# An LSTM with a conditioned adapter: its largest weight loaded by GpSimd in eight 1 MB transfers, x loaded a block earlier

## The chip, the cores and the metric

The kernel runs on one core of a Trainium2 chip. The metric is the device time of one execution in microseconds (us). An execution under the profiler leaves a trace, whose span is given beside its own time. Engines are named as in the profile: PE is TensorE's matmul (PEld its weight load), DVE VectorE, ACT ScalarE, POOL GpSimd, SP SyncE, which only issues transfers here. A "q" behind a name (SPq) is the engine's sequencer.

## What is computed

x is 16 sequences of 256 steps of 256 numbers, all float32. An LSTM with a start state `cond` runs over it and is added to x; then an adapter whose low-rank weights are made from `cond` is added to that.

```
xz = x @ Wx + b                       # (16, 256, 1024), all steps at once
for t in 0..255:                      # the recurrence
    i, f, o, g = split(xz[:, t] + h @ Wh)
    c = sigmoid(f) * c + sigmoid(i) * tanh(g)
    h = sigmoid(o) * tanh(c)
x = x + all h
c = layernorm(cond) * gamma + beta    # 16 x 256
hid = gelu(c @ W1 + bias1)            # 16 x 256
a1, b1, a2, b2 = split(hid @ W2 + bias2)   # W2 is 256 x 8192; each a 16 x 256 x 8 set
mid = gelu(x @ base_down + (x . a2) . b2)
out = x + mid @ base_up.T + a1 . (b1 . mid)
```

## The kernel before

Each engine runs a program of its own, written out by hand; semaphores join them. The 256 time steps are cut into 32 blocks of 8. A block k does three things at once.

- The recurrence: per step PE adds `h @ Wh` to the seeded gate sums (`z`, `z_o`, L712: 24 matmuls), DVE turns them (L868, L872), ACT takes the tanh of the gates (L422, L428), DVE makes cell and hidden state (L878 to L893). Each needs the one before; the second `h_t` instruction (L893, from `z_o`) ends a step.
- The projection `x @ Wx` for block k+2, in eight matmul pieces (`project`, L502) that PE runs in the idle time of the steps; the table `PIECES` says how many are done before each step of blocks 0, 1 and later ones. DVE adds the bias (`evacuate_projection`, L802), and SP rearranges the result into `seed` with four transfers (`load_seed`, L255). x for it is loaded by SP (`load_x`, L244), turned by PE (`transpose_x`, L483) and copied by ACT (`evacuate_x`, L352).
- The adapter for an earlier block (from block 3 on; L515 to L592).

The adapter's weights are made in the first four blocks by `make_weights`, one copy of which stands in the program of PE, of ACT and of DVE. Layer norm of `cond`, then in block 0 at step 3 `c @ W1` and the GELU that makes `hid`, in steps 4 and 5 base_up is turned. W2 (8.4 MB) is cut into four quarters, which are a2, b1, b2 and a1 in the order in which they are made (`QUARTERS`). From step 11 on, each step multiplies one of a quarter's four parts (L633), so a quarter takes four steps; `w2_loaded` says that its data are there. There are three buffers for the four quarters, so the last one waits for the first one's products (`w_psum`). DVE adds the bias (L920, `w_biased`), and GpSimd carries each finished quarter to its place across partitions with four small transfers (`place_w`, L1020), for which PE waits (`w_placed`) in steps 18 and 22 to turn a2 and b1 (L645), and in block 3 to use b2 and a1.

Before, SP loads W2 (`load_w2`, L272 to L283): 16 pieces in two halves of 64 partitions and 256 KB, in runs of 1 KB, and each half waits until the third one before it has landed (`UNDER_WAY`), so that at most three are under way. SP's order by block:

```
k = 0: W2 pieces 0, 1;  x(3);  W2 pieces 2 to 7, a bias transfer behind four of them;  seed(2)
k = 1: x(4);  W2 pieces 8 to 12;  seed(3)
k = 2: x(5);  W2 pieces 13 to 15;  seed(4)
k > 2: x(k+3);  seed(k+2);  a store
```

GpSimd makes constants, adds h to x once per block (`add_h`, L1001) and places the weights; it issues no loads.

Of the kernel before, what the change touches and what calls it, by code (L numbers as in the profile page):

```python
# [42 lines left out]
UNDER_WAY = 3  # L43
# [9 lines left out]
PIECES = ((0, 0, 0, 2, 2, 4, 5, 7, 8), (0, 1, 2, 3, 4, 5, 6, 7, 8), (0, 1, 2, 3, 4, 5, 6, 7, 8))  # L53
# [5 lines left out]
def lstm_adapter(nc, x, cond, Wx, Wh, b, base_up, base_down, gamma, beta, W1, bias1, W2, bias2, out):  # L59
    ctx = ExitStack()  # L60
    with ctx:
# [36 lines left out]
        w1 = sb("w1", [P, 2, D])  # L98
# [50 lines left out]
        w2_loaded = [[[sem(f"w2_loaded{q}_{i}_{r}") for r in range(2)] for i in range(NQ)] for q in range(4)]  # L149
# [89 lines left out]
        def _(sp):  # L239
# [30 lines left out]
            w2_parts = W2.rearrange("(k p) (q j h n) -> q h k p j n", p=P, q=4, j=NQ, n=W_HALF)  # L270

            def load_w2(piece):  # L272

                n, i = divmod(piece, NQ)
                q, (h, kc) = QUARTERS[n], divmod(i, 2)
                if piece == 3 * NQ:
                    sp.wait_ge(w_psum, 2)
                for r, rows in enumerate((slice(0, P // 2), slice(P // 2, P))):
                    back, half = divmod(2 * piece + r - UNDER_WAY, 2)
                    if back >= 0:  # L280
                        sp.wait_ge(w2_loaded[QUARTERS[back // NQ]][back % NQ][half], 16)
                    sp.dma_start(w2[q][rows, kc, :].rearrange("p (j h n) -> p h j n", j=NQ, n=W_HALF)[:, h],
                                 w2_parts[q, h, kc, rows]).then_inc(w2_loaded[q][i][r], 16)  # L283

            bias_q = bias2.rearrange("(q j n) -> j q n", q=4, j=NQ)

            def load_w_bias(j):
                sp.wait_ge(w_bias_zeroed, 1)
                sp.dma_start(w_bias[32 * j:32 * j + B, :, :], bias_q[j].partition_broadcast(B)).then_inc(w_bias_loaded, 16)

# [13 lines left out]
            sp.dma_start(b1_col[:, :], bias1.rearrange("(k p) -> p k", p=P),  # L304
                         allow_slow_non_contiguous=True).then_inc(w_loaded["w1"], 16)
# [4 lines left out]
            def one_block(k, front):  # L310
                if not k.at_least(1):
                    load_w2(0)
                    load_w2(1)
                if k.plus(3).exists():
                    load_x(k.plus(3))
                for piece in {0: range(2, 8), 1: range(8, 13), 2: range(13, 4 * NQ)}.get(k.k, ()):
                    load_w2(piece)
                    if 2 <= piece < 2 + NQ:
                        load_w_bias(piece - 2)
# [19 lines left out]
        def _(act):  # L339
# [40 lines left out]
            def make_weights(k, s):  # L380

                if k == 0 and s == 3:

                    act.wait_ge(w_loaded["w1"], 32)
# [28 lines left out]
            def one_block(k, front):  # L413
                a, e, done = follower(k), early(k), follower(k.plus(-1))
                for s in range(TB):
# [34 lines left out]
                    if s == 1 and not k.at_least(1):  # L450
                        evacuate_x(k.plus(2))
# [26 lines left out]
        def _(pe):  # L478
# [115 lines left out]
            def make_weights(k, s):  # L594
# [7 lines left out]
                if k == 0 and s == 3:  # L602
                    pe.wait_ge(w_loaded["w1"], 32)
                    pe.wait_ge(cond_t_ready, 1)
                    for i in range(2):
                        for kc in range(2):
                            ins = pe.matmul(aux[:, i * B:(i + 1) * B], w1[:, kc, i * P:(i + 1) * P], c_t[:, kc, :],
                                            start=(kc == 0), stop=(kc == 1))
                    ins.then_inc(hidden_psum, 1)
# [9 lines left out]
                if 0 <= k * TB + s - W_FIRST < 4 * NQ:  # L619
# [9 lines left out]
                    for half in w2_loaded[q][i]:  # L629
                        pe.wait_ge(half, 16)  # L630
# [44 lines left out]
            project(Blk(0, 1), range(6))  # L675
# [5 lines left out]
            def one_block(k, front):  # L681
# [3 lines left out]
                for s in range(TB):  # L685
# [111 lines left out]
        def _(dve):  # L797
# [63 lines left out]
            for q in range(XQ - 1):  # L861
# [34 lines left out]
            def make_weights(k, s):  # L896
# [14 lines left out]
                if 0 <= u < 2 * NQ and not between:  # L911
                    n, h = divmod(u, 2)
                    dve.wait_ge(w_psum, u + 1)
                    if u == 0:
                        dve.wait_ge(w_bias_loaded, 16 * NQ)
# [13 lines left out]
            def one_block(k, front):  # L929
                a, e, f, done = follower(k), early(k), k.plus(2), follower(k.plus(-1))  # L930
                for s in range(TB):
# [25 lines left out]
                    if s == 0 and not k.at_least(1):  # L957
                        evacuate_projection(Blk(0, 1), XQ - 1)
# [25 lines left out]
        def _(pool):  # L984
# [27 lines left out]

            places = {0: a1_t[:, :], 1: w_tmp[:, 1, :], 2: w_tmp[:, 0, :], 3: b2_t[:, :]}
# [10 lines left out]
            def one_block(k, front):  # L1024
                add_h(k)
                for n in {0: (0,), 1: (1, 2), 2: (3,)}.get(k.k, ()):
                    place_w(n)

# [24 lines left out]
```

## Time and profile before

| | us |
|---|---|
| median of 3 runs | 602.32 (600.86 to 602.75) |
| the profiled execution, its own time | 606.49 |
| its span | 604.7 |
| PE busy in the span | 584.7 (97%); 14116 matmul and 14116 weight-load instructions |
| DVE, ACT, POOL busy | 502.5, 384.6, 47.4 |
| mean granted clock of TensorE | 0.994 |

Times of the trace are microseconds from the start of the span. In rows of instructions the first number is the start, the second the time that the merged instructions took, then engine, line, operation and tiles (out<-in); in brackets the idle time of the engine before it and what ended it. In rows of windows each engine has its busy time and its number of instructions; PEclk is the granted share of TensorE's clock, the DMA share the mean busy share of the 16 DMA engines.

### The profile page before, as it was taken

Reading aid. Unit: us, or ns where it says so; the run is one execution under the profiler, and the core shown is the slowest. Engines: PE = TensorE matmul, PEld = TensorE weight load, DVE = VectorE, ACT = ScalarE, POOL = GpSimd, SP = SyncE. Lnnn points to the kernel's source line nnn. Section 1 sums busy time; section 2 is a strip of 40 time slices with the busy share of each in tenths; the row PEclk is TensorE's granted clock in tenths of the full one; section 3 lists DMA queues with packets and bytes.
Section 4 is the critical chain, followed back from the end, with each engine's and each line's share of the span. In section 5 each row is a group of like instructions: output and inputs, shape, how many; then the busy total and the mean of one; then the engine's idle time right before and its main releaser. Section 6 shows DMA issues by size and latency. Waiting matters only on the chain.

```text
span 604.7 us, 34273 instructions
## 1 busy us (share of the span) xinstructions
PE 584.7 (97%) x14116; PEld 440.1 (73%) x14116; DVE 502.5 (83%) x2810; ACT 384.6 (64%) x2155; POOL 47.4 (8%) x91
## 2 busy tenths in 40 slices
PE   8888989999999999999999999999999999999997
PEld 7555557777777777777777777777777777777886
DVE  4667768888888888888888888888888888888874
ACT  2555546666666666666666666666666666666663
POOL 4002122000000000000000000000000000000000
PEclk9989899999999999999999999999999999999999
DMA  7999872123332212323221132332123333212201
GB/s 195 184 179 179 174 148 45 33 37 56 56 56 56 41 27 48 55 56 56 56 42 37 37 55 57 55 56 40 40 35 56 55 56 55 45 37 26 56 21 29
DMA packets 40158, 39.75 MB, mean 66 GB/s; under 512 B 4369, under 2 KB 38977, under 8 KB 40002
## 3 DMA queue, kind: packets, MB, share of 16 engines
q1 hardware_dynamic: 39456, 37.01, 33.7%
q8 instruction: 112, 1.84, 1.4%
q0 software_dynamic: 512, 0.53, 0.5%
q14 instruction: 44, 0.36, 0.3%
q10 hardware_dynamic: 34, 0.02, 0.0%
HBM read 16.05 MB, written 4.19 MB: 33 GB/s over the span
## 4 chain that ended last, share of the span: by engine, by line
PE 93%; DVE 2%; issue 2%; DMA 2%; SPq 0%; ACT 0%; DVEq 0%; ACTq 0%
PE z L712 35%; PE x_bank L502 18%; PE z_o L712 9%; PE aux L531 8%; PE out_bank L558 7%; PE aux L515 3%; PE aux L483 2%; PE out_bank L590 2%; PE aux L538 2%; PE out_bank L633 1%; DMA x_nat<-in_x 1%; DMA seed<-proj 1%; PE out_bank L579 1%; PE x_bank L579 1%; PE x_bank L531 0%
## 5 line engine op out<-in xcount | busy, mean ns | idle before, releaser
L712 PE MATMUL z<-wh,h_t 128*16 128x96 f32 x8160 | 235.5, 249 | 5.4 <-issue 3.4
L712 PEld LDWEIGHTS z<-wh,h_t 128*16 128x16 f32 x8160 | 154.2, 96 | 110.6 <-DVE h_t L893 79.8
L868 DVE STREAM_TRANSPOSE z<-z 128x96 f32<-128x96 f32 x512 | 152.4, 298 | 71.1 <-PE z L712 47.8
L422 ACT ACTIVATE gates<-z 128x48 f32<-128x48 f32 x512 | 108.1, 211 | 122.5 <-DVE z L868 122.3
L502 PE MATMUL x_bank<-wx,x_t 128*128 128x256 f32 x512 | 153.6, 387 | 0.6 <-ACT x_t L352 0.5
L358 ACT ACTIVATE z<-seed 128x96 f32<-128x96 f32 x512 | 126.9, 248 | 4.2 <-DMA seed<-proj 4.2
L712 PE MATMUL z_o<-wh,h_t 128*16 128x64 f32 x4080 | 105.6, 220 | 4.9 <-issue 4.9
L878 DVE SCALAR_TENSOR_TENSOR prod<-gates 128x32 f32<-128x32 f32 x512 | 98.2, 192 | 0.3
L712 PEld LDWEIGHTS z_o<-wh,h_t 128*16 128x16 f32 x4080 | 80.7, 97 | 5.4 <-issue 5.3
L502 PEld LDWEIGHTS x_bank<-wx,x_t 128*128 128x128 f32 x512 | 79.1, 192 | 4.2 <-ACT x_t L352 0.7
L428 ACT ACTIVATE gate_o<-z_o 128x32 f32<-128x32 f32 x256 | 50.6, 198 | 31.7 <-DVE z_o L872 6.4
L362 ACT ACTIVATE z_o<-seed 128x64 f32<-128x64 f32 x256 | 58.3, 228 | 19.3
L872 DVE STREAM_TRANSPOSE z_o<-z_o 128x64 f32<-128x64 f32 x256 | 65.7, 257 | 5.1 <-PE z_o L712 5.0
L1001 POOL TENSOR_TENSOR xp<-x_t,h_t 128x128 f32<-128x128 f32 (+1 forms) x60 | 30.3, 527 | 473.7 <-DVE h_t L893 456.6
L434 ACT ACTIVATE z_o<-z 128x16 f32<-128x16 f32 x256 | 43.0, 168 | 25.6
L802 DVE TENSOR_TENSOR proj<-x_bank,b_all 128x256 f32<-128x256 f32 x128 | 54.0, 422 | 2.4 <-PE x_bank L502 2.3
L883 DVE SCALAR_TENSOR_TENSOR z<-prod 128x16 f32<-128x16 f32 x256 | 46.7, 182 | 8.7
L888 DVE SCALAR_TENSOR_TENSOR gates<-prod 128x32 f32<-128x32 f32 x255 | 46.9, 184 | 0.0
L434 ACT ACTIVATE tanc<-tanc 128x16 f32<-128x16 f32 x256 | 45.6, 178 | 0.0
L893 DVE SCALAR_TENSOR_TENSOR h_t<-gate_o,z_o 128x16 f32<-128x16 f32 x256 | 43.7, 171 | 0.1
L893 DVE SCALAR_TENSOR_TENSOR h_t<-gate_o,tanc 128x16 f32<-128x16 f32 x256 | 43.7, 171 | 0.0
L531 PE MATMUL aux<-xp,down 128*128 128x128 f32 x232 | 43.3, 289 | 0.0
(137 smaller groups left out, 521.9 us busy)
## 6 DMA issues: line engine op xcount, KB each, us to landing
seed<-proj SPq DMA_DIRECT2D x128, 128.0 KB, 4.4
w<-in_L_cond_W SPq DMA_DIRECT2D x33, 256.0 KB, 4.8
x_nat<-in_x SPq DMA_DIRECT2D x32, 128.0 KB, 4.1
out<-y_nat SPq DMA_DIRECT2D x32, 128.0 KB, 4.1
wx<-in_L_cond_Wx SPq DMA_DIRECT2D x2, 256.0 KB, 3.9
wx<-in_L_cond_Wx SPq DMA_DIRECT2D x1, 512.0 KB, 4.8
wh<-in_L_cond_Wh SPq DMA_DIRECT2D x2, 256.0 KB, 5.7
wh<-in_L_cond_Wh SPq DMA_DIRECT2D x1, 512.0 KB, 6.0
```

The lines of the kernel that those rows point to most:

```text
L358: act.activation(z_bank[m][:, 0:GC], seed[buf][:, s, P * m:P * m + GC], ACT.Copy)\
L362: act.activation(o_bank[:, 0:OC].rearrange("p (m c) -> p m c", c=C), seed[buf][:, s, :].rearrange("p (m q) -> p m q", m=NM)[:, :, GC:P], A ...
L422: act.activation(gates[s % 2][m][:, 0:3 * B].rearrange("p (g b) -> p g b", b=B), zt[m].rearrange("p (g c) -> p g c", c=C)[:, :, 0:B], ACT. ...
L434: act.activation(tanc[m], cell[m], ACT.Tanh, scale=0.5).then_inc(tanc_ready[m], 1)
L502: ins = pe.matmul(x_bank[q % 2][:, 0:XW].rearrange("p (m g c) -> p m g c", m=NM, c=C), x_t[f.k % N_X][:, kc, :], wx[:, kc, :].rearrange("p ...
L531: ins = pe.matmul(mid_bank[a.lane][:, cols], lhs, rhs, start=(part == 0), stop=(part == 2))
L712: ins = pe.matmul(dst, h_prev[:, kc, :], rhs, start=False, stop=(kc == 1), skip_group_check=True)
L802: dve.tensor_tensor(proj[f.par][:, q * XW:(q + 1) * XW], x_bank[q % 2][:, 0:XW], b_all[:, q * XW:(q + 1) * XW], ALU.add).then_inc(xz_ready, 1)
L868: dve.transpose(zt[m], z_bank[m][:, 0:GC]).then_inc(turned[m], 1)
L872: dve.transpose(zt_o, o_bank[:, 0:OC]).then_inc(turned_o, 1)
L878: dve.scalar_tensor_tensor(prod[m][:, :], now[:, 0:2 * B], 1.0, now[:, 2 * B:4 * B], ALU.add, ALU.mult).then_inc(prod_ready[m], 1)
L893: dve.scalar_tensor_tensor(h_t[k.par][:, m, s, 0:B], gate_o[:, B * m:B * (m + 1)], 1.0, tanc[m], ALU.add, ALU.mult).then_inc(ht_ready[m], 1)
```

## The change

W2 goes from SP to GpSimd. There are eight transfers of 1 MB, two (one per half of `hid`) for each quarter, in runs of 8 KB; the source has an outer count of 8: row `8 b + a` of a half of W2 goes to partition `16 a + b`. GpSimd waits for the seeds of block 0 and then issues six of them, each behind a bias transfer, which is cut into 8 partitions each (eight transfers where there were four); the last two bias transfers follow, and the two W2 transfers of the last quarter come behind the placing of the first one, without a small one. PE waits for a whole quarter at once. Because the rows of W2 change their partitions, the columns of `hid` must too: ACT writes a copy of W1 with its columns in that order (`w1_turned`, block 0, step 2), and the bias column `b1_col` is loaded in that order by two transfers.

SP, without W2 and its waits, loads x for block 2 ahead of the seeds of block 0, and from block 0 on x for block k+4 instead of k+3. All eight pieces of block 1's projection are done ahead of step 0, block 2's x is turned in step 0 instead of step 1, and block 2's pieces are spread over steps 1 to 7 as the table says.

```
-UNDER_WAY = 3
-PIECES = ((0, 0, 0, 2, 2, 4, 5, 7, 8), (0, 1, 2, 3, 4, 5, 6, 7, 8), (0, 1, 2, 3, 4, 5, 6, 7, 8))
+PIECES = ((0, 0, 2, 3, 3, 4, 5, 7, 8), (0, 1, 2, 3, 4, 5, 6, 7, 8), (0, 1, 2, 3, 4, 5, 6, 7, 8))
...
SP:
-            w2_parts = W2.rearrange("(k p) (q j h n) -> q h k p j n", p=P, q=4, j=NQ, n=W_HALF)
-            def load_w2(piece):
...
-            def load_w_bias(j):
...
+            load_x(Blk(0, 0, 2))
             load_seed(Blk(0, 0))
-            load_x(Blk(0, 0, 2))
...
                 if not k.at_least(1):
-                    load_w2(0)
-                    load_w2(1)
-                if k.plus(3).exists():
                     load_x(k.plus(3))
-                for piece in {0: range(2, 8), 1: range(8, 13), 2: range(13, 4 * NQ)}.get(k.k, ()):
-                    load_w2(piece)
...
+                    load_x(k.plus(4))
+                elif k.plus(4).exists():
+                    load_x(k.plus(4))
ACT:
+                if k == 0 and s == 2:
+                    act.wait_ge(w_loaded["w1"], 48)
+                    halves = "p k (i a b) -> p (k i) a b"
+                    act.activation(w1_turned[:, :, :].rearrange(halves, i=2, a=8),
+                                   w1[:, :, :].rearrange("p k (i b a) -> p (k i) a b", i=2, a=8), ACT.Copy)\
+                       .then_inc(w1_ready, 1)
...
-                    if s == 1 and not k.at_least(1):
+                    if s == 0 and not k.at_least(1):
                         evacuate_x(k.plus(2))
PE:
-                    for half in w2_loaded[q][i]:
-                        pe.wait_ge(half, 16)
+                    if i == 0:
+                        pe.wait_ge(w2_loaded[q], 32)
...
-            project(Blk(0, 1), range(6))
+            project(Blk(0, 1), range(N_PIECES))
...
                             if s == 0:
-                                project(Blk(0, 1), range(6, N_PIECES))
-                            if s == 1:
                                 transpose_x(f, both)
POOL:
+            bias_q = bias2.rearrange("(q j n) -> j q n", q=4, j=NQ)
+            w2_q = W2.rearrange("(k b a) (q n) -> q k a b n", k=2, a=8, q=4)
+            def load_w_bias(i):
+                first = 32 * (i // 2) + B // 2 * (i % 2)
+                pool.dma_start(w_bias[first:first + B // 2, :, :], bias_q[i // 2].partition_broadcast(B // 2))\
+                    .then_inc(w_bias_loaded, 16)
+            def load_w2(n, kc):
+                q = QUARTERS[n]
+                pool.dma_start(w2[q][:, kc, :], w2_q[q, kc]).then_inc(w2_loaded[q], 16)
+            pool.wait_ge(seed_loaded[0], 16 * NQ)
+            for i in range(2 * (NQ - 1)):
+                load_w_bias(i)
+                load_w2(i // 2, i % 2)
+            for i in range(2 * (NQ - 1), 2 * NQ):
+                load_w_bias(i)
...
                 for n in {0: (0,), 1: (1, 2), 2: (3,)}.get(k.k, ()):
                     place_w(n)
+                if k.k == 0:
+                    pool.wait_ge(w_psum, 2)
+                    for kc in range(2):
+                        load_w2(NQ - 1, kc)
```

SP's queue in block 0 before, from the load of base_down on (`w_0` and `w_1` are buffers of W2):

```order
L267 DMA down<-in_L_cond_base_down 128x2x256
L282 DMA w_0<-in_L_cond_W 64x4x256 x3
L282 DMA w_0<-in_L_cond_W 64x4x256 [waits w2_loaded2_0_0]
L244 DMA x_nat<-in_x 128x1x256 [waits xt_psum]
L282 DMA w_0<-in_L_cond_W 64x4x256 [waits w2_loaded2_0_1]
L282 DMA w_0<-in_L_cond_W 64x4x256 [waits w2_loaded2_1_0]
L289 DMA w_bias<-in_L_cond_bias 16x4x512 [waits w_bias_zeroed]
```

The same place in the changed kernel, up to the x of block 1's turn:

```order
L267 DMA down<-in_L_cond_base_down 128x2x256
L244 DMA x_nat<-in_x 128x1x256 [waits xt_psum] x2
L255 DMA seed<-proj 16x8x256 [waits seeded_o,xz_ready,seeded1,seeded0]
L255 DMA seed<-proj 16x8x256 [waits xz_ready] x3
L244 DMA x_nat<-in_x 128x1x256 [waits xt_psum]
```

All W2 and bias transfers have left the queue with their waits, and two loads of x stand together where one did.

GpSimd's program in the changed kernel, from the step of the layer norm that stood right ahead of `add_h` (`xp_early`) before, to the end of block 0:

```order
L989 TENSOR_TENSOR c_stat<-c_stat,neg_half 16x1 [waits ln_step,w_bias_zeroed]
L996 DMA w_bias<-in_L_cond_bias 8x4x512 [waits seed_loaded0]
L1001 DMA w_0<-in_L_cond_W 128x1x2048
...
L996 DMA w_bias<-in_L_cond_bias 8x4x512 x2
L979 TENSOR_TENSOR xp_early<-x_t,h_t 128x128 [waits ht_ready0,xt_ready]
L979 TENSOR_TENSOR xp_early<-x_t,h_t 128x128 [waits ht_ready1]
L1017 DMA w_tmp<-w_nat 128x1x64 [waits w_biased]
L1017 DMA w_tmp<-w_nat 128x1x64 x3
L1001 DMA w_0<-in_L_cond_W 128x1x2048 [waits w_psum]
L1001 DMA w_0<-in_L_cond_W 128x1x2048
```

Where "..." stands, the pair of a bias and a W2 transfer comes five times more; the first placing (`w_tmp`) and the last quarter of W2 share this queue with them.

## Rows read from the trace of the kernel before

**Rows 1.** The page's 40 slices of the span, busy tenths of PE and DMA
```profile
PE   8888989999999999999999999999999999999997
...
DMA  7999872123332212323221132332123333212201
```

**Rows 2.** DVE in order of time: the second h_t instruction of some steps
```profile
19.36 0.17 DVE L893 SCALAR_TENSOR_TENSOR h_t<-gate_o,z_o 128x16 f32<-128x16 f32 x1
38.78 0.17 DVE L893 SCALAR_TENSOR_TENSOR h_t<-gate_o,z_o 128x16 f32<-128x16 f32 x1
41.59 0.17 DVE L893 SCALAR_TENSOR_TENSOR h_t<-gate_o,z_o 128x16 f32<-128x16 f32 x1
57.47 0.17 DVE L893 SCALAR_TENSOR_TENSOR h_t<-gate_o,z_o 128x16 f32<-128x16 f32 x1
62.63 0.17 DVE L893 SCALAR_TENSOR_TENSOR h_t<-gate_o,z_o 128x16 f32<-128x16 f32 x1
65.78 0.17 DVE L893 SCALAR_TENSOR_TENSOR h_t<-gate_o,z_o 128x16 f32<-128x16 f32 x1
83.09 0.17 DVE L893 SCALAR_TENSOR_TENSOR h_t<-gate_o,z_o 128x16 f32<-128x16 f32 x1
102.31 0.17 DVE L893 SCALAR_TENSOR_TENSOR h_t<-gate_o,z_o 128x16 f32<-128x16 f32 x1
119.91 0.17 DVE L893 SCALAR_TENSOR_TENSOR h_t<-gate_o,z_o 128x16 f32<-128x16 f32 x1
```

**Rows 3.** The chain that ended last, 0 to 110 us: start, us, what
```profile
29.11 0.86 issue
...
35.10 2.38 issue
...
58.94 2.52 issue
...
78.62 2.53 issue
```

**Rows 4.** DMA queues: packets, MB, share; the whole span, then 16 to 90 us
```profile
q8 instruction: 112, 1.84, 1.4%
...
q1 hardware_dynamic: 13026, 12.35, 88.5%
...
q8 instruction: 12, 0.20, 1.4%
```

**Rows 5.** Windows between the stalls: PE, PEld, DVE, ACT, POOL, clock, DMA share, GB/s
```profile
37.47:58.94 21.47, 20.23 (x503) 13.10 (x504) 17.40 (x96) 12.49 (x73) 3.56 (x7) 0.92 0.97 175
61.46:78.62 17.16, 17.16 (x376) 10.30 (x375) 14.36 (x74) 9.81 (x55) 2.09 (x4) 0.90 0.94 185
```

**Rows 6.** Windows behind the second and the third stall
```profile
38.66:42.00 3.34, 3.28 (x59) 2.29 (x62) 2.30 (x14) 2.16 (x12) 1.01 (x2) 0.50 0.79 148
62.50:65.90 3.40, 3.40 (x58) 2.31 (x50) 2.54 (x14) 1.65 (x10) 0.00 (x0) 0.51 0.71 162
```

**Rows 7.** Windows of the first loads and of the stretch that loads W2
```profile
0.00:10.00 10.00, 8.94 (x42) 8.17 (x42) 3.77 (x13) 3.02 (x5) 5.98 (x10) 1.00 0.75 240
...
17.00:87.00 70.00, 59.20 (x1443) 39.58 (x1444) 51.02 (x275) 37.48 (x213) 9.47 (x18) 0.95 0.95 181
```

**Rows 8.** ACT in order of time: the first seed
```profile
16.83 0.42 ACT L358 ACTIVATE z<-seed 128x96 f32<-128x96 f32 x2 [4.16 <-DMA seed<-proj]
```

**Rows 9.** POOL and PE in order of time: the first placing, its use
```profile
56.39 2.24 POOL L1020 DMA_DIRECT2D w_tmp<-w_nat  x4 [16.54 <-DVE w_nat L920]
...
68.58 0.44 PE L645 MATMUL aux<-ident,w_tmp 128*128 128x128 f32 x2
```

**Rows 10.** PE in order of time: x for block 4 is turned
```profile
56.64 0.44 PE L483 MATMUL aux<-ident,x_nat 128*128 128x128 f32 x2 [0.36 <-DMA x_nat<-in_x]
```

**Rows 11.** ACT in order of time: a copy of 128x512, step 3's first gates
```profile
8.28 0.63 ACT L399 ACTIVATE wh<-wh 128x512 f32<-128x512 f32 x1 [2.98 <-DMA wh<-in_L_cond_Wh]
...
25.03 0.21 ACT L422 ACTIVATE gates<-z 128x48 f32<-128x48 f32 x1 [0.71 <-DVE z L868]
```

More of the change, by code:

```diff
@@ L97, in lstm_adapter @@
         c_t = sb("c_t", [P, 2, B])
-        w1 = sb("w1", [P, 2, D])
+        w1, w1_turned = sb("w1", [P, 2, D]), sb("w1_turned", [P, 2, D])
         b1_col = sb("b1_col", [P, 2])
@@ L148, in lstm_adapter @@
                     ("wx_g", "wx_if", "wx_o", "wh_g", "wh_if", "wh_o", "b", "down", "up", "ln", "cond", "w1")}
-        w2_loaded = [[[sem(f"w2_loaded{q}_{i}_{r}") for r in range(2)] for i in range(NQ)] for q in range(4)]
+        w1_ready = sem("w1_ready")
+        w2_loaded = [sem(f"w2_loaded{q}") for q in range(4)]
         w_bias_zeroed, w_bias_loaded = sem("w_bias_zeroed"), sem("w_bias_loaded")
@@ L268, in load_cols @@
                   .then_inc(w_loaded[name], 16)
-            w2_parts = W2.rearrange("(k p) (q j h n) -> q h k p j n", p=P, q=4, j=NQ, n=W_HALF)
-            def load_w2(piece):
[L274 to L285, printed above, removed]
-            def load_w_bias(j):
-                sp.wait_ge(w_bias_zeroed, 1)
-                sp.dma_start(w_bias[32 * j:32 * j + B, :, :], bias_q[j].partition_broadcast(B)).then_inc(w_bias_loaded, 16)
             load_x(Blk(0, 0))
@@ L300, in _ @@
             sp.dma_start(c_beta[:, :], beta.partition_broadcast(B)).then_inc(w_loaded["ln"], 16)
+            load_x(Blk(0, 0, 2))
             load_seed(Blk(0, 0))
-            load_x(Blk(0, 0, 2))
             sp.dma_start(w1[:, :, :], W1.rearrange("(k p) n -> p k n", p=P)).then_inc(w_loaded["w1"], 16)
-            sp.dma_start(b1_col[:, :], bias1.rearrange("(k p) -> p k", p=P),
-                         allow_slow_non_contiguous=True).then_inc(w_loaded["w1"], 16)
+            for kc in range(2):
+                sp.dma_start(b1_col[:, kc:kc + 1], bias1.rearrange("(k b a) -> k a b", k=2, a=8)[kc],
+                             allow_slow_non_contiguous=True).then_inc(w_loaded["w1"], 16)
             load_cols(up_raw, base_up, 0, 0, D, "up")
@@ L380, in make_weights @@
             def make_weights(k, s):
+                if k == 0 and s == 2:
[4 more added lines that the diff above has]
+                       .then_inc(w1_ready, 1)
                 if k == 0 and s == 3:
-                    act.wait_ge(w_loaded["w1"], 32)
+                    act.wait_ge(w_loaded["w1"], 48)
                     act.wait_ge(hidden_psum, 1)
@@ L602, in make_weights @@
                 if k == 0 and s == 3:
-                    pe.wait_ge(w_loaded["w1"], 32)
+                    pe.wait_ge(w1_ready, 1)
                     pe.wait_ge(cond_t_ready, 1)
@@ L606, in make_weights @@
                         for kc in range(2):
-                            ins = pe.matmul(aux[:, i * B:(i + 1) * B], w1[:, kc, i * P:(i + 1) * P], c_t[:, kc, :],
+                            ins = pe.matmul(aux[:, i * B:(i + 1) * B], w1_turned[:, kc, i * P:(i + 1) * P], c_t[:, kc, :],
                                             start=(kc == 0), stop=(kc == 1))
@@ L859, in _ @@
             dve.tensor_scalar(c_stat[:, 3:4], c_stat[:, 2:3], 1.0 / D, LN_EPS, ALU.mult, ALU.add).then_inc(ln_step, 1)
-            for q in range(XQ - 1):
+            for q in range(XQ):
                 evacuate_projection(Blk(0, 1), q)
@@ L914, in make_weights @@
                     if u == 0:
-                        dve.wait_ge(w_bias_loaded, 16 * NQ)
+                        dve.wait_ge(w_bias_loaded, 2 * 16 * NQ)
                     if h == 0 and n >= 2:
@@ L956, in one_block @@
                         add_residual(done)
-                    if s == 0 and not k.at_least(1):
-                        evacuate_projection(Blk(0, 1), XQ - 1)
                     if front and k.at_least(1) and s in EVACUATE_AT:
@@ L1027, in one_block @@
                     place_w(n)
+                if k.k == 0:
+                    pool.wait_ge(w_psum, 2)
+                    for kc in range(2):
+                        load_w2(NQ - 1, kc)
             schedule(one_block)
```

2 lines of the change are left out of this document (removed).

## The prediction

> **What bounds the kernel now.** First I read the 40 slices [rows 1]. TensorE is busy 9 tenths or more from the seventh slice on and 7 to 9 tenths before; the DMA engines are near full exactly in those first six slices, about 90 us. So there are two stretches, and the change touches only the first.
>
> Then I counted steps. The second h_t row of a step ends it. Blocks end at 38.78, 57.47, 83.09, 102.31 and 119.91 [rows 2]. The last block took 17.60 us, 2.20 per step: that is the recurrence itself, PE, DVE and ACT in turn, and no change of loads can shorten it. Against it blocks 1, 2 and 3 (18.69, 25.62 and 19.22 us) are over by 1.1, 8.0 and 1.6, and the seven steps from 19.36 to 38.78 (19.42, at 2.20 each 15.4) by 4.0. In all **14.7 us** stand above the steady pace; more cannot be won after the first step.
>
> The chain says what most of it is [rows 3]: four pieces called issue, 0.86, 2.38, 2.52 and 2.53 us, **8.29** together. PE waits for nothing there that the profile shows, always inside the step's matmuls. I read them as waits for code. 
>
> A stall also costs afterwards: right after the second and third one TensorE ran at 0.50 of its clock for 3.3 us, that is at 1.2 instead of 2.4 GHz [rows 6]. The steps in it took 41.59 - 38.78 = 2.81 and 65.78 - 62.63 = 3.15 [rows 2], 0.6 and 0.95 too long; with an estimate of 0.45 for what spills into the steps behind them I count **2.0**.
>
> **The change part by part.** (1) *W2 leaves SP's queue.* The 32 pieces of 256 KB go; eight of 1 MB come, on GpSimd, with an outer count of 8 and, for six of them, a bias transfer of 8 partitions ahead. If this keeps W2 on one part of the engines and code on another, the stalls and the slow clock go: -8.29 - 2.0. I keep 0.5 of it, since the seeds, W1 and base_up still precede the first code packets on all engines: **-9.8**. No row tells which engine a packet used; this is the assumption that the forecast stands on, and its ends are 0 and -10.3.
>
> The Trainium skill (DMA: Bandwidth & Descriptors, Rules for kernel authors) says that an outermost count c under 16 confines a transfer to at most c engines, and advises against it. No run here shows it yet. By it W2 gets half the engines and the sum is the 598.2 below; were it on all of them, the wait of 2.0 would go, and with it the assumption that code is kept apart.
>
> (2) *Does W2 still come in time?* Nothing in the trace loads W2 on part of the engines, so I bound it. High: the first 10 us moved 240 GB/s at a share of 0.75, 320 when full; half of that is 160. Low: 17 to 87 moved 181 at 0.95 [rows 7]; half is 95. GpSimd starts when seed 0 has landed, 16.83 [rows 8]; an issue costs 2.24/4 = 0.56 us [rows 9], 14 of them 7.8, over by 25 and far ahead of add_h(0) at 38.8, so nothing waits behind them on GpSimd. At 160 three quarters (6.29 MB) take 39.3 us from 17.9, to 57.2; the same engines carry half of the 1.7 MB of seeds, x and base_down, 5 us more: quarters land at about 33, 48 and 62.5. At 2.2 a step from 19.5 they are needed at steps 11, 15 and 19: 41.5, 50.3 and 59.1. The placing of a2 queues behind them on GpSimd's queue, and PE wants it 2.6 us after the end of step 17 (68.58 against 65.95) [rows 2, 9], then at 59.5. So at 160 the third quarter is late by about 3; at 95 it lands at 84 + 5, late by 30; were it on all engines, 0. W2's runs are 8 KB, the longest in the kernel, so it is nearest the first row and rather above it; I take **+2.0**. Quarter 3 goes out behind that placing (53); half of it behind the third quarter lands near 69, needed at 67.9 + 2: no term, but no slack either.
>
> (3) *x earlier.* x for block 4 stood behind two blocks of W2 waits on SP, and PE waited 0.36 for it at 56.64 [rows 10]. Now it goes before block 0's end: **-0.2**, ends 0 and -0.36. x for block 2 moves ahead of seed 0 on SP; SP waits there for the first projection, so one more issue delays nothing.
>
> (4) *Projection evened out.* Two matmuls and one DVE addition leave step 0 for the prologue, where PE idles for seed 0 until 16.83 [rows 8]; block 2's eight pieces spread over steps 1 to 7. Steps 1 to 7 stand 4.0 above their pace, the first two stalls are 0.86 + 2.38 of it, and 0.8 is left [rows 2, 3]; I take **-0.5** of that, ends 0 and -0.8. Should the last addition come late, it can hold the first turn by its own length and no more.
>
> (5) *W1 is turned on ACT.* A copy of 128x512; the like one took 0.63 [rows 11]. ACT idles 0.71 before the next gates [rows 11], but must end early for the same turn: **+0.2**, ends 0 and 0.6. W1 is issued right behind seed 0, which lands at 16.83, two steps earlier. The bias column as two transfers: no one waits, 0.
>
> Sum: 606.49 - 9.8 + 2.0 - 0.2 - 0.5 + 0.2 = **598.2 us**. The profiled execution is 4.2 above the median of 602.32; steady steps cannot differ that much, so I take it that stalls differ between executions, that the others have one or two fewer, and that without stalls all come out alike. Against the median that is 4.1 us, 0.7%.
>
> **The rivals.** *A, slower: code shares its engines with W2.* Nothing limits what is under way any more: GpSimd queues 6.29 MB at once where SP kept three pieces. If code fetches meet that queue, every packet of code is late, not one in three. 8.4 MB at 160 take 52 us, to about 70; PE needs a packet every 21.47/4 = 5.4 us [rows 5], so nine in that time. Nine stalls of 2.5 plus 0.9 of slow clock are 31, less the 10.3 of now: 606.5 + 20 = 626; with five of nine 606.5 + 17 - 10.3 = 613. It decides as soon as more than three packets are late. For it: PE stalls only beside W2. Against: the spacer transfers look like steering, but that is no row.
>
> *B, W2 late.* The rate is nearer 95 than 160: PE waits in steps 15 to 23 instead. Without a wait the sum is 596.2, so it decides from a wait of about 6 us, a rate near 150, against the median; at 120 the three quarters end at 75, 16 late: 596.2 + 16 = 612. For it: no row above 320 in full.
>
> *C, nothing moves.* Code is late for the seeds and x, not W2, or the number of stalls stays. Only (3) and (4) remain: 602.3 - 0.5 = 601.8. The Trainium skill (same page, Queues, rings and completion order) says that an engine goes round its queues packet by packet, so that depth does not matter. The trace does not bear it out alone: four stalls beside W2, none in 518 us without.
>
> *D, all of it.* No wait for W2, and what block 2 has over beside stalls and slow clock (8.0 - 5.05 - 1.25 = 1.7) goes in good part too: 596.2 down to 594.5, and 592.5 with every other end.
>
> **How the numbers follow.** The forecast, with W2 late by 0 to 4 (596.2 to 600.2), 0.45; D 0.15. A 0.18, C 0.13, B 0.09 (a third of it still faster). 0.3% is 1.8 us, about what a measurement tells from no change: under 600.5 is faster: 0.45 + 0.15 + 0.03 = 0.63. Same (C, and edges of B): 0.14. Slower: 0.23. The range runs from D's 592.5 to 609, which takes in C and the near parts of A and B and leaves about 0.18 above.
>
> **What would show it.** Right: no issue piece of over 1 us in the chain before 90 us; clock 1.00 throughout; block 2 under 20 us; SP free of W2; PE's L633 matmuls waiting 0 to 4 us in step 18 or 19. Wrong: issue pieces every 5 us between 18 and 70 (A); a wait for W2 or the placed weights over 6 us (B); four pieces as now (C).

## The result and the profile after

| | before | after |
|---|---|---|
| median, us | 602.54 (600.86 to 604.28) | 645.57 (642.66 to 647.96) |
| ratio of after to before | | 1.071, 95% interval 1.066 to 1.077 |
| span of the profiled execution | 604.7 | 646.2 |
| mean granted clock of TensorE | 0.994 | 0.962 |

The change is **43 us slower**, and the prediction of 598.2 with its range up to 609 was wrong. The 40 slices of after (16 us each), against [rows 1]: PE, its clock, the DMA engines.

```profile
PE   8746255899999999999999999999999999999997
...
PEclk9977768799999999999999999999999999999999
DMA  6975539521232323232222333323332212323211
```

The loss lies in slices 2 to 8. TensorE has time over in all of them, and the DMA engines in all but the second and the seventh, where they are 9 tenths busy. The second h_t rows on DVE end the first step, block 0, steps 12 and 13 (counted from 0), and blocks 1, 2 and 3, against [rows 2]:

```profile
20.65 0.17 DVE L873 SCALAR_TENSOR_TENSOR h_t<-gate_o,z_o 128x16 f32<-128x16 f32 x1
48.98 0.17 DVE L873 SCALAR_TENSOR_TENSOR h_t<-gate_o,z_o 128x16 f32<-128x16 f32 x1
67.39 0.17 DVE L873 SCALAR_TENSOR_TENSOR h_t<-gate_o,z_o 128x16 f32<-128x16 f32 x1
88.60 0.17 DVE L873 SCALAR_TENSOR_TENSOR h_t<-gate_o,z_o 128x16 f32<-128x16 f32 x1
94.69 0.17 DVE L873 SCALAR_TENSOR_TENSOR h_t<-gate_o,z_o 128x16 f32<-128x16 f32 x1
124.11 0.17 DVE L873 SCALAR_TENSOR_TENSOR h_t<-gate_o,z_o 128x16 f32<-128x16 f32 x1
143.49 0.17 DVE L873 SCALAR_TENSOR_TENSOR h_t<-gate_o,z_o 128x16 f32<-128x16 f32 x1
```

The first step ends 1.3 us later than before; the seven steps behind it took 28.3 (19.4 before), block 1 45.7 (18.7), block 2 29.4 (25.6), block 3 19.4 (19.2): 41.2 in all. Step 13 alone took 21.2 (the expectations below, which were written earlier, call it step 12). PE in order of time says where it stood (in brackets the idle time before the row):

```profile
37.80 0.98 PE L694 MATMUL z<-wh,h_t 128*16 128x96 f32 x17 [7.40 <-issue]
...
47.68 0.40 PE L694 MATMUL z_o<-wh,h_t 128*16 128x64 f32 x11 [3.50 <-issue]
...
51.27 0.66 PE L465 MATMUL aux<-ident,x_nat 128*128 128x128 f32 x2 [3.18 <-DMA x_nat<-in_x]
...
59.70 0.60 PE L694 MATMUL z<-wh,h_t 128*16 128x96 f32 x19 [1.40 <-issue]
...
87.26 1.05 PE L615 MATMUL out_bank<-w,hid 128*16 128x256 f32 x8 [18.10 <-DVE w_nat L900]
...
115.64 1.16 PE L694 MATMUL z<-wh,h_t 128*16 128x96 f32 x24 [8.26 <-issue]
```

Three losses: waits called issue, 7.40 + 3.50 + 1.40 + 8.26 = **20.6** where before had 8.29 [rows 3]; one wait of **18.1** for DVE's addition of the bias to the first of W2's products; 3.2 for x. With the first step that is 12.3 + 18.1 + 3.2 + 1.3 = 34.9 of 41.2. The rest, 6.3, I put down to the steps behind these waits; it is a remainder, not measured step by step. In the windows after three of them the granted clock was 0.50, that is 1.2 GHz (columns as in [rows 5]).

```profile
37.80:40.60 2.80, 2.80 (x38) 2.26 (x38) 1.83 (x11) 1.29 (x8) 0.00 (x0) 0.50 0.54 125
...
87.30:90.00 2.70, 2.44 (x48) 1.43 (x52) 1.93 (x12) 1.50 (x10) 0.00 (x0) 0.50 0.01 3
...
115.60:118.00 2.40, 2.36 (x42) 1.82 (x41) 1.35 (x9) 0.90 (x6) 0.00 (x0) 0.50 0.37 46
```

What DVE waited for in step 13 is not W2 itself but the bias, issued on GpSimd behind it. DVE in order of time, and the DMA issues between 17 and 120 us (KB each, median us to landing):

```profile
86.61 0.59 DVE L900 TENSOR_TENSOR w_nat<-out_bank,w_bias 128x256 f32<-128x256 f32 x1 [19.05 <-DMA w_bias<-in_L_cond_bias]
```

```profile
w<-in_L_cond_W POOLq DMA_DIRECT2D x8, 1024.0 KB, 21.2
...
w_bias<-in_L_cond_bias POOLq DMA_DIRECT2D x8, 64.0 KB, 17.7
x_nat<-in_x SPq DMA_DIRECT2D x4, 128.0 KB, 26.4
```

x takes 26.4 us to land. Two windows, one while the first six W2 transfers are on their way, one while the last quarter comes:

```profile
40.00:84.00 44.00, 20.20 (x424) 13.12 (x422) 13.98 (x79) 10.96 (x61) 0.99 (x2) 0.73 0.53 137
96.00:116.00 20.00, 10.98 (x264) 6.18 (x267) 11.01 (x53) 6.99 (x40) 4.06 (x8) 0.84 1.04 128
```

In the first the engines are busy half of the time, as an outer count of 8 on 16 engines would have it, and move 137 GB/s where before moved 181 [rows 7]. W2 alone was slower still: the sixth transfer was issued at 24.8, and the slowest one landed 61.4 us after its issue, which puts the end of the third quarter at about 86. As an estimate, 6.29 MB from 19.1 to 86 are 94 GB/s. In the second window the share is full, yet the rate is no higher.

### The profile page after: what moved, and what is told of

The parts are those of the page before. It is cut to its first block, busy times and chain, and to the rows that moved or that the text cites. A ratio compares the mean times of both kernels' runs of the same rounds, so it can differ in the third digit from the quotient of the medians.

```text
span 646.2 us, 34241 instructions
## 1 busy us (share of the span) xinstructions
PE 591.6 (92%) x14116; PEld 444.2 (69%) x14116; DVE 503.7 (78%) x2810; ACT 385.3 (60%) x2156; POOL 56.7 (9%) x107
## 4 chain that ended last, share of the span: by engine, by line
PE 86%; DMA 5%; another core or an unknown queue 3%; DVE 3%; issue 2%; POOL 0%; SPq 0%; ACT 0%; DVEq 0%
PE z L694 32%; PE x_bank L484 17%; PE z_o L694 8%; PE aux L513 8%; PE out_bank L540 6%; DMA x_nat<-in_x 5%; PE aux L497 3%; PE aux L465 2%; PE out_bank L572 2%; PE aux L520 2%; PE out_bank L615 1%; PE out_bank L561 1%; PE x_bank L561 1%; PE x_bank L513 0%
## 5 line engine op out<-in xcount | busy, mean ns | idle before, releaser
L694 PE MATMUL z<-wh,h_t 128*16 128x96 f32 x8160 | 237.5, 251 | 19.9 <-issue 17.1
L484 PE MATMUL x_bank<-wx,x_t 128*128 128x256 f32 x512 | 156.1, 392 | 1.0 <-ACT x_t L328 0.5
L484 PEld LDWEIGHTS x_bank<-wx,x_t 128*128 128x128 f32 x512 | 80.6, 196 | 5.1 <-issue 1.3
## 6 DMA issues: line engine op xcount, KB each, us to landing
w<-in_L_cond_W POOLq DMA_DIRECT2D x8, 1024.0 KB, 21.2
```

Source lines behind the costliest of these rows:

```text
L484: ins = pe.matmul(x_bank[q % 2][:, 0:XW].rearrange("p (m g c) -> p m g c", m=NM, c=C), x_t[f.k % N_X][:, kc, :], wx[:, kc, :].rearrange("p ...
L694: ins = pe.matmul(dst, h_prev[:, kc, :], rhs, start=False, stop=(kc == 1), skip_group_check=True)
```

## The experiments

These waits also hold later packets, such as the one behind the 8.26 of after, which lagged 9.9 while the last quarter came. The kernel before measured 602.5 beside after and 603.6 to 604.7 beside the others, so rows of different sets compare to within 1 or 2 us.

| kernel | median us | W2 on | queued at most, runs | lags, us | issue |
|---|---|---|---|---|---|
| before | 602.5 | SP | 3 x 256 KB, 1 KB | 3.1, 4.6, 2.6, 1.7, 2.3 | 8.3 |
| after | 645.6 | GpSimd | 6 x 1 MB, 8 KB, outer 8 | 10.1, 7.0, 9.4, 1.0, 0.5 | 21.0 |
| e1 | 637.0 | GpSimd | the same | 9.5, 7.1, 6.4, 1.0, 1.1 | 20.5 |
| e2 | 650.8 | GpSimd | the same, other order | 8.1, 2.3, 0.4, 5.3, 6.8 | 17.2 |
| e3 | 623.1 | GpSimd | 6 x 1 MB, 8 KB, outer 16 | 7.0, 8.1, 7.4, 7.3, 1.4 | 19.2 |
| e4 | 603.2 | SP | 3 x 256 KB, 1 KB | 2.5, 1.8, 0.9, 2.5, 1.8 | 1.8 |
| e5 | 639.5 (one run) | GpSimd | as after, and the bias on SP | 11.3, 8.3, 22.0, 1.6, 0.6 | 23.3 |
| e6 | 618.0 | GpSimd | 24 x 256 KB, 2 KB | 6.5, 7.4, 6.8, 5.9, 1.5 | 14.1 |
| e7 | 624.1 | GpSimd | 1 x 1 MB, 8 KB | 8.0, 2.3, 1.6, 5.5, 4.6 | 11.4 |
| v1 | 613.6 | GpSimd | 3 x 256 KB, 1 KB | 7.7, 2.3, 1.1, 4.0, 2.1 | 8.0 |
| e8 | 626.4 | SP | 6 x 1 MB, 8 KB | 8.4, 7.6, 6.6, 6.9, 1.1 | 16.3 |
| e9 | 622.1 | SP | 8 x 256 KB, 1 KB | 5.1, 8.5, 6.9, 6.3, 1.2 | 19.2 |
| v2 | 606.8 | SP | 3 x 256 KB, 1 KB | 2.7, 1.7, 1.9, 1.3, 2.0 | 1.0 |
| e10 | 614.5 | SP | 2 x 256 KB, 1 KB | 1.7, 1.8, 2.5, 1.0, 0.6 | 0.7 |

In e3, e6, e8 and e9 the first three quarters have landed before the last of these packets is fetched.

**e1_bias_ahead**: the last two bias transfers go ahead of W2.

```
             pool.wait_ge(seed_loaded[0], 16 * NQ)
+            for i in range(2 * (NQ - 1), 2 * NQ):
+                load_w_bias(i)
             for i in range(2 * (NQ - 1)):
                 load_w_bias(i)
                 load_w2(i // 2, i % 2)
-            for i in range(2 * (NQ - 1), 2 * NQ):
-                load_w_bias(i)
```

> The change with one move: the last two bias transfers are issued ahead of the six W2 transfers instead of behind them. The profile of the change shows DVE waiting 19.1 us in step 12 for a bias landing and PE 18.1 us with it. Theory: that transfer only stood behind three quarters of W2 in GpSimd's queue. Then that wait is gone, but W2 itself still comes at about 112 GB/s, so the third quarter lands near 86 and is waited for by 3 to 6 us in steps 18 to 19: 645.6 - 18 + 5, about 633 us. Rival (the wait is W2's own slow rate, the bias only shows it): the same wait turns up at the next W2 use and the time stays within 4 us of 645.6.

Measured: 637.0. DVE's wait for the bias is 15.3 instead of 19.1 (us in total, times, the longest), so the theory's "that wait is gone" missed: five W2 transfers still stand ahead of the sixth bias transfer.

```profile
DVE w_nat L900 <- DMA w_bias<-in_L_cond_bias: 15.3, 1, 15.3
```

This fits order on that queue as the cause of this wait, and moving two of eight cures little of it; e5 takes the bias off that queue.

**e2_other_half**: each W2 transfer ahead of its bias transfer, which is meant to put W2 on the other half of the engines.

```
             for i in range(2 * (NQ - 1)):
-                load_w_bias(i)
                 load_w2(i // 2, i % 2)
+                load_w_bias(i)
```

> The change with each W2 transfer ahead of its bias transfer instead of behind it; by the completion counts of the change W2 ran on eight of sixteen engines, and this order should put it on the other eight. Theory 1 (code packets use one fixed engine, and W2 sat on its half): code stalls (20.6 us in the change) fall to under 5 us, time about 620. Theory 2 (one fixed engine, on the free half, and the stalls have another cause): code stalls rise or stay, 645 or more. Theory 3 (code packets go round all engines): about as much stall in other places, 640 to 650, with the packets that were late now on time and those that were on time late. The bias wait of step 12 stays in all cases, since two bias transfers are still last.

Measured: 650.8, just over theory 3's 640 to 650. Of the five packets in the table, those that had been late at 961 and 1217 are now on time, those on time at 1473 and 1729 are late. The first, at 705, was late both times; all engines were busy there (share 1.14 from 24 to 34.5 us in after, 1.09 from 24 to 30 in e2), so it says nothing on halves. PE in order of time:

```profile
35.57 0.98 PE L694 MATMUL z<-wh,h_t 128*16 128x96 f32 x17 [5.19 <-issue]
54.08 0.66 PE L465 MATMUL aux<-ident,x_nat 128*128 128x128 f32 x2 [11.12 <-DMA x_nat<-in_x]
68.90 0.34 PE L694 MATMUL z<-wh,h_t 128*16 128x96 f32 x2 [3.04 <-issue]
88.14 1.06 PE L615 MATMUL out_bank<-w,hid 128*16 128x256 f32 x8 [14.62 <-DVE w_nat L900]
```

So code isn't tied to one part of the engines: with the engines half busy (share 0.53 in after and 0.56 in e2, from 40 to 84 us), W2 meets some of its packets in either order. The records don't name a packet's engine, so that W2 changed halves and that code goes round all engines are the readings that fit, not rows.

**e3_outer16**: 8 becomes 16 in all four views of W2, W1 and the bias column.

```
-            w2_q = W2.rearrange("(k b a) (q n) -> q k a b n", k=2, a=8, q=4)
+            w2_q = W2.rearrange("(k b a) (q n) -> q k a b n", k=2, a=16, q=4)
```

> The change with an outer count of 16 instead of 8 for W2 (and with it W1's and bias1's order); everything else is left. Theory (the outer count halves the engines, and the halved engines hold up bias, x and code): W2 comes at twice the 112 GB/s, three quarters end near 18 + 6.3/0.22 = 47 instead of 86, the bias wait of step 12 (wanted near 46) falls from 18 to about 2 us and x is no longer half late; code stalls stay as in the kernel before or worse: 605 to 622 us. Rival (1 MB transfers of 8 KB runs from GpSimd are slow as such): rate within 20% of 112 GB/s, 635 us or more.

Measured: 623.1, just over the theory's 605 to 622. A window of it, and PE's waits called issue:

```profile
24.00:56.00 32.00, 19.71 (x413) 14.12 (x415) 14.20 (x80) 12.81 (x67) 2.27 (x5) 0.87 1.03 211
```

```profile
PE z L694 <- issue: 13.5, 4, 4.1
PE z_o L694 <- issue: 4.4, 1, 4.4
PE x_bank L484 <- issue: 1.2, 1, 1.2
```

211 GB/s, no wait for bias or x, but code is late at every edge while W2 is loading, 19.2 us in all. The outer count alone costs after 645.6 - 623.1 = **22.5**; nearly all of that is data, since the waits for code fell by 1.8 only.

**e4_x_and_proj**: the kernel before with the early x and the evened projection alone (`PIECES`, `load_x`, `project` as in the change; W2, bias and W1 as before).

> The kernel before with only the earlier loads of x and the evened projection; W2 stays on SP as it was. Theory (this part is harmless, all of the loss is W2's): 0 to 1.5 us faster than before, 601 to 602.5. Rival (it has a share in the loss, through the first step that ended 1.3 us later in the change): 1 to 3 us slower, 603.5 to 605.5.

Measured: 603.2, ratio 0.999 (0.996 to 1.002). This half of the change is harmless and worth nothing that shows. Code was on time (1.8 us of waits), and ACT waited for seeds behind SP's W2 instead:

```profile
ACT z L361 <- DMA seed<-proj: 9.9, 3, 4.2
```

The longest of the three, 4.2, is the wait for the first seed, which before has too [rows 8]; the late ones are the other two, 3.38 and 2.31, 5.7 together.

**e5_bias_on_sp**: after, with the bias loaded by SP ahead of base_down; the small GpSimd transfers fill a tile that nobody reads.

```
+            for j in range(NQ):
+                sp.dma_start(w_bias[32 * j:32 * j + B, :, :], bias_rows[j].partition_broadcast(B))\
+                  .then_inc(w_bias_loaded, 16)
             load_cols(down, base_down, 0, 0, D, "down")
...
-                pool.dma_start(w_bias[first:first + B // 2, :, :], bias_q[i // 2].partition_broadcast(B // 2))\
-                    .then_inc(w_bias_loaded, 16)
+                pool.dma_start(spare[first:first + B // 2, :, :], bias_q[i // 2].partition_broadcast(B // 2))\
+                    .then_inc(spaced, 16)
```

> SP loads the bias for real, in four transfers ahead of base_down; the eight small GpSimd transfers stay where they are but fill a tile that nobody reads. Theory: the 18.1 us that DVE and PE lose in step 12 are one wait for the last bias transfers, whose completion comes only when the W2 ahead of them has passed (the runs so far: 645.6, and 637.0 with four of the six W2 ahead of them gone). Then this wait is gone, some of it comes back as waits for the third quarter and for the placed a2 (at about 112 GB/s, 9.4 MB with the spacers from 19 us on end past 85, against step 19 near 75), 3 to 9 us; the code stalls stay. About 633, 628 to 638. Rival: W2 itself is what step 12 waits for, and the bias only the last of two; then PE waits elsewhere for as long and the time stays over 641.

Measured: 639.5 in the profiled execution, 650.7 in the other; no ratio can be given. Step 13 is back at 2.2 us, so the bias was what it waited for. But PE now waits longer for x, and for code, 23.3 in all:

```profile
65.20 0.66 PE L472 MATMUL aux<-ident,x_nat 128*128 128x128 f32 x2 [15.18 <-DMA x_nat<-in_x]
```

```profile
PE z L701 <- issue: 9.8, 2, 8.2
PE z_o L701 <- issue: 5.1, 1, 5.1
PE aux L634 <- issue: 4.7, 1, 4.7
PE x_bank L491 <- issue: 3.6, 2, 3.3
```

The theory's 628 to 638 missed: x and code are late in the bias's place, on SP's queue and on q8. That was the rival's course, though what step 13 had waited for was the bias. (The expectation's "four of the six" gone in e1 is a slip: one of six was.)

**e6_runs_2k** and **e7_one_under_way** change e3 in one size each: e6 cuts each megabyte into four transfers with runs of 2 KB, e7 issues one megabyte at a time, with all bias transfers ahead of the first.

```
e6:
-                pool.dma_start(w2[q][:, kc, :], w2_q[q, kc]).then_inc(w2_loaded[q], 16)
+                for c in range(0, D * RANK, W_COLS):
+                    pool.dma_start(w2[q][:, kc, c:c + W_COLS], w2_q[q, kc][:, :, c:c + W_COLS]).then_inc(w2_loaded[q], 16)
e7:
+                if kc == 1:
+                    pool.wait_ge(w2_loaded[q], 16)
+                elif n > 0:
+                    pool.wait_ge(w2_loaded[QUARTERS[n - 1]], 32)
                 pool.dma_start(w2[q][:, kc, :], w2_q[q, kc]).then_inc(w2_loaded[q], 16)
```

> As the run with an outer count of 16 (623.1, 19.2 us of code stalls, one at each edge of a code packet), but each 1 MB of W2 is four transfers of 256 KB in runs of 2 KB in place of 8 KB; as much data stands queued at once. Theory P: a code packet waits for the long packets being moved (8 KB each), so with packets of a quarter the stalls fall under 8 and the time comes to about 610. Theory Q: it waits for the depth of what is queued, which is the same; the stalls stay at 17 to 21 and the time within 5 of 623.

> As the run with an outer count of 16 (623.1), but GpSimd issues a W2 transfer of 1 MB only when the one before it has landed, and all bias transfers ahead of the first. Runs stay 8 KB. Theory Q, depth: with one transfer queued the code stalls fall from 19.2 to 5 to 8 and the time comes to about 610; W2 is slower by the gap between landing and next issue, some 2 us of each 6 to 7, so that its third quarter may be late by up to 5. Theory P, packet size: the stalls stay at 15 to 20 and the time at 618 to 628.

Measured: 618.0 and 624.1, issue waits 14.1 and 11.4 from 19.2. Neither theory is right as put. Shorter runs leave the lags at 5.9 to 7.4. A single megabyte leaves some at 1.6 and others at 4.6 to 8.0. The 8.0 falls where bias and base_down are queued too, as v1's 7.7 does; but the 5.5 also stopped PE, for 3.1 us, so one such transfer can already be too much. What e7 gained on code it lost elsewhere: PE waited 5.2 us for placed weights and 4.5 for x_t, and DVE 5.0 for `add_h` (xp_early), since GpSimd's other work now stands behind its waits for W2.

**v1_pool_pieces**: e4, with `load_w2` in its old pieces and its limit of three moved to GpSimd, the bias on SP.

```
SP:
+            for j in range(NQ):
+                load_w_bias(j)
             load_cols(down, base_down, 0, 0, D, "down")
POOL:
+                for piece in {0: range(0, 8)}.get(k.k, ()):
+                    load_w2(piece)
                 add_h(k)
+                for piece in {0: range(8, 12), 1: range(14, 16)}.get(k.k, ()):
+                    load_w2(piece)
...
+                for piece in {0: range(12, 14)}.get(k.k, ()):
+                    load_w2(piece)
```

> The kernel before with the early x and the evened projection, and with W2 issued by GpSimd, in SP's old halves of 256 KB (runs of 1 KB, all engines) with at most three under way; the bias goes on SP. It leaves out what the other runs showed to cost time: the outer count of 8, the bias behind W2, the deep queue of 8 KB packets. SP no longer waits for W2 ahead of seeds. Theory: code stalls as in the kernel before or fewer (2 to 8 us), no wait for a seed in steps 15 to 25, no wait for the bias; 596 to 601, about 599. Rival: what is queued sets the code stalls whoever issues it, and the seeds only wait elsewhere: 601 to 605, the same as before.

Measured: 613.6, ratio 1.016 (1.009 to 1.022), a miss. PE waited 8.0 for code and 5.3 for placed weights, which on GpSimd stand behind waits for W2. The lag of 7.7, at the same limit of three as e4, falls where the bias and base_down are queued at once on SP; that they cause it is only a reading. So moving W2 to GpSimd was no gain even in the old pieces.

**e8_sp_queue**: e3 with W2 issued by SP, unhindered, behind its x loads.

```
SP:
+                for n in {0: range(NQ - 1), 1: (NQ - 1,)}.get(k.k, ()):
+                    if n == NQ - 1:
+                        sp.wait_ge(w_psum, 2)
+                    for kc in range(2):
+                        load_w2(n, kc)
                 if front:
                     load_seed(k.plus(2))
```

> As the run with an outer count of 16 (623.1; code packets began 7.0 to 8.1 us after TensorE entered the packet before, 19.2 us of stalls), but SP issues W2, behind its loads of x, in the same 1 MB transfers with nothing holding them back; the bias transfers stay on GpSimd. In the kernel before, where SP issued W2 in 256 KB with three under way, code packets began 1.4 to 5.2 us after. Theory S: it is GpSimd's queue that code waits for; on SP's the delays fall to 2 to 5 and the time to 602 to 610. Theory D: what is queued in all decides, whoever issues it; the delays stay at 6 to 9 and the time at 618 to 628. In both, the seeds behind six unhindered transfers could come late, with a wait of up to 5 us at the end of block 1.

Measured: 626.4, lags 6.6 to 8.4 while W2 loads: theory D. It isn't GpSimd's queue that code waits for.

**v2_seed_first**: e4 with SP's seeds ahead of the last pieces of W2 in each block.

```
-                for piece in {0: range(2, 8), 1: range(8, 13), 2: range(13, 4 * NQ)}.get(k.k, ()):
+                for piece in {0: range(2, 6), 1: range(8, 11), 2: range(13, 15)}.get(k.k, ()):
                     load_w2(piece)
...
                 if front:
                     load_seed(k.plus(2))
+                for piece in {0: range(6, 8), 1: range(11, 13), 2: range(15, 16)}.get(k.k, ()):
+                    load_w2(piece)
```

> The kernel before with the early x and the evened projection (603.2, level with the kernel before), and SP's order changed so that the seeds of blocks 2, 3 and 4 go ahead of the last two, two and one pieces of W2 of their block; they went behind all of them, and steps 15, 23 and 25 ran 3.45, 2.7 and 2.1 us long there. Theory: these three steps come back to 2.2 to 2.6, W2 is not late for it (each quarter's last piece has about 10 us in hand), code stalls 2 to 8: 595 to 600, about 597.5. Rival: the freed steps only bring the need for W2 forward, and PE waits for W2 or its placing instead: 601 to 604.

Measured: 606.8, ratio 1.004 (1.002 to 1.007), a miss: the rival's course, and 2.8 over its 601 to 604. The seeds are no longer late (the one wait of 4.2 is that for the first seed), and PE waits for W2 in their place:

```profile
PE out_bank L638 <- DMA w<-in_L_cond_W: 7.6, 4, 4.0
```

**e9_eight_under_way** and **e10_two_under_way** change one number of e4.

```
-UNDER_WAY = 3
+UNDER_WAY = 8      (e9)
+UNDER_WAY = 2      (e10)
```

> The kernel before with the early x and the evened projection (603.2; code packets began 0.9 to 2.7 us after TensorE entered the packet before, two short stalls), but SP keeps up to eight transfers of 256 KB of W2 under way in place of three. Runs stay 1 KB, queue, engines and the order of the issues stay. Theory D, the amount queued sets how late code comes: with 2 MB under way the delays grow to 6 to 9 as in the runs with 1 MB transfers, PE stalls at three to five edges for 2 to 4 us each: 610 to 620. Theory P, only long packets hold code up: the delays stay under 5, W2 is earlier and SP free sooner, so that the seeds that ACT waited 9.9 us for come in time: 596 to 602.

> The same with two transfers of 256 KB under way in place of three. Theory D: code comes at least as early as with three (delays up to 2.7), no stall over 1 us; what is left is W2's rate, which falls by up to a third (181 GB/s to 120 to 150 with its gaps), so that PE waits for W2 in steps 15 to 26: 606 to 618. Theory P: the same for the waits, code unchanged. A time under 601 would say that three are too many, and neither expects it.

Measured: 622.1, ratio 1.025 (1.016 to 1.033), and 614.5, 1.015 (1.009 to 1.022). The first is theory D's course, 2 over its 610 to 620; the second is within the forecast. PE's waits in e9, then ACT's for seeds (the first seed's 4.2 in it) and DVE's in e10:

```profile
PE z L715 <- issue: 12.0, 4, 4.1
PE z_o L715 <- issue: 6.2, 1, 6.2
```

```profile
ACT z L361 <- DMA seed<-proj: 12.3, 3, 5.3
```

```profile
DVE w_nat L921 <- PE out_bank L636: 3.5, 3, 2.0
DVE w_nat L921 <- DMA w_bias<-in_L_cond_bias: 3.4, 1, 3.4
```

And windows over the loading in e9 and in e10:

```profile
24.00:62.00 38.00, 23.61 (x504) 16.25 (x505) 18.80 (x107) 15.25 (x87) 1.00 (x2) 0.87 1.12 195
```

```profile
20.00:100.00 80.00, 62.89 (x1520) 41.52 (x1520) 54.17 (x297) 39.91 (x227) 9.93 (x19) 0.94 0.74 153
```

This shows a cause of the code stalls. With runs, queue, engines and order unchanged, eight under way instead of three bring the lags from 0.9 to 2.5 up to 5.1 to 8.5 while W2 loads, and cost 622.1 - 603.2 = 19 us: about what e3 lost. Each against the kernel before of its own set, it is 18, and the interval of e9's ratio leaves 10 to 20. Two under way free code almost entirely (0.7 us of waits) and cost 11 in late W2, bias and seeds. Of the counts tried, three is the best; no version here beats the kernel before. The limit on W2 does not set the lag alone: at three it was up to 2.5 in e4, 4.6 in before and 7.7 in v1, where other transfers are queued beside W2.

**The sum.** From after to e3, the outer count: 22.5 us. From e3 to e4, all that is left of W2's move: 19.9. From e4 to before: under 1. The three differences add up to 43 by construction; what speaks for the middle one as the price of the missing limit is that e9 gives 18 to 19 for the depth alone.

## Why the prediction was wrong

- **Step (1), W2 leaves SP's queue, -9.8: the step that failed.** Its assumption was that W2 on one part of the engines leaves code alone. In after itself, with the engines half busy, two packets lagged 7.0 and 9.4 us, and in e2, with the order turned, two others 5.3 and 6.8: half the engines are no shield. And the same step threw away what did protect code, `UNDER_WAY`. Issue waits went from 8.3 to 20.6, not to 0.5. Rival A named this mechanism (nothing limits what is under way) but had its price wrong, many stalls of 2.5 us; there are four, of 1.4 to 8.3 (7.40 + 3.50 + 1.40 + 8.26), since a packet behind W2 comes 7 to 10 us after PE starts the piece before.
- **Step (2), does W2 come in time, +2.0: mis-sized.** I dated the three quarters and not the bias transfers that stand behind all of them on the same queue, which the first addition needs; they cost 18.1. I took 160 GB/s between bounds of 95 and 160. The stretch moved 137 with seeds and x in it, and W2 alone came at the low bound: some 94, its third quarter in at about 86 (62.5 at 160, 89 at 95). PE did not wait for that quarter itself, since the bias, x and code held it for longer. Rival B (612) had W2 late by its rate, but at waits of its own, and smaller.
- **Step (3), x earlier, -0.2: turned round by (1).** x had to pass W2: a load issued at 20.3 landed at 51.1, and PE waited 3.2 us for it in after, 11.1 in e2, 15.2 in e5. Without W2's move (e4) the earlier x does no harm.
- **Step (4), projection evened out, -0.5: not confirmed.** Together with (3) 0.999 (0.996 to 1.002) in e4; a gain of 0.5 lies inside that.
- **Step (5), W1 turned on ACT, +0.2: not confirmed.** Step 3 took 2.36 before and 2.58 in after, just the forecast; but in e4 and e9, which have no such copy, it took 3.00 and 2.76.
- **The reading of before was right in the main**: the issue waits stand at the edges of code packets, and W2 holds these up. A slow clock followed the second and the third [rows 6], not the first and the fourth (1.00 from 30 to 33 and from 81.2 to 84.5).
- **Two slips of the sums** change nothing: rival C's -0.5 is (3), (4) and (5) together, (3) and (4) alone make -0.7; and the ends that are named give D 593.3, not 592.5.

The outer count behaved as the Trainium skill (DMA: Bandwidth & Descriptors, Rules for kernel authors) has it: under 16, a transfer has that many engines at most. The traces agree: DMA share 0.53 and 137 GB/s at 8, 1.03 and 211 at 16. I drew from it that code is kept apart, which e2 does not bear out, and left out that everything else on those engines has to pass W2: x took 26.4 us to land in after, 15.0 in e3.

Rival C leant on depth not mattering. The Trainium skill (DMA: Bandwidth & Descriptors, Queues, rings and completion order) says that an engine goes round its queues, draining one packet of about 9 to 17 descriptors before it switches; that depth does not matter was my conclusion from it. The runs don't fit a wait that is free of depth: at 1 KB runs the lag grew from at most 2.5 to 8.5 us with the count under way alone, while 8 KB runs in e3 gave no longer lags (7.0 to 8.1) than 1 KB runs in e9.

## What to carry to other kernels

A limit on the transfers under way that looks like a brake on bandwidth may be what lets the engine's own code through: count the bytes queued per DMA engine, and date the arrival of every code packet against it, before removing the limit. When a load is moved, date what stands behind it on the same queue and engines too, down to the smallest transfer: here bias transfers of 64 KB cost 18.1 us, more than the 12.3 of added code stalls.
